# A post-norm decoder layer on one core: who asks for the early loads, whose queue the emptying copies use, and a new order of steps

## The chip, the cores and the metric

One core of a Trainium2 chip. The time is device microseconds from start to end of one launch. Engines: TensorE (PE; PEld is its weight load), VectorE (DVE), ScalarE (ACT), GpSimd (POOL) and SyncE (SP). SP and ACT can both ask the DMA engines for transfers; POOL does so for the indirect ones.

## What is computed

A decoder layer over x of 16 batches x 100 rows x 256 columns: self-attention with rotary turns, cross-attention to the first rows of a context of 16 x 361 x 256, and a mixture of 14 experts with one expert for each row; each part is added to its input and normalised.

```python
x = _layernorm(x + attn(x, qkv_w, qkv_b, out_w, out_b))              # 16 heads of 16, rotary
x = _layernorm(x + xattn(x, ctx, ctx, WQ, bQ, WK, bK, WV, bV, WO, bO, lens))   # 16 heads of 64, causal and padded
x = _layernorm(x + moe(x, router_w, w1, b1, w2, b2))                 # argmax of 14, exact gelu, 256 -> 512 -> 256
```

## The kernel before

The 1,600 rows are cut in two ways: 16 batches b of 100 rows for attention, and 13 tiles t of 125 rows (the last has 100) for loads, projections and norms. Two blocks follow each other. The first does both attentions, the router, and scatters every finished row with its gate and its number to its expert's place in a table in device memory, `expert_rows` (15 x 1,664 rows of 258 words). The second, `experts_block`, loads 128 rows for each expert from that table, runs the two projections and scatters the result to the output.

In the first block the order of all work is a list of 1,715 step names, `STEPS`, written out by hand or by a planner (line 81). Each engine walks the same list (`for step in PLAN: do(step)`), does the steps that are its own and skips the others, so the list fixes the order on each engine; between engines only semaphores wait. Names used below: `xT.t` (PE) turns tile t of x, `xT_hi.t` (ACT) and `xT_lo.t` (DVE) take it as a high and a low part; `w_hi.k` (ACT), `w_lo_v.k` (DVE) or `w_lo_p.k` (POOL) split weight piece k the same way (0, 1: qkv; 2: out; 3, 4: W_K; 5, 6: W_V; 7, 8: W_Q, not split; 9, 10: W_O); `cT.b` turns the context; `v.b`, `qk.t`, `qkT.t`, `K.g.n`, `V.b.c`, `Q.g.n`, `out.t`, `wo.t` are projections and turns on PE; `scores`, `max`, `exp`, `inv`, `norm`, `turn`, `copy_a` or `copy_v` (ACT or DVE), `pv`, `o_hi` (ACT), `o_lo` (DVE) are the steps of attention with side s (self) or x (cross), batch and half; `ln.s.t` ends the self norm of tile t; `x_load.t` and `c_load.b` (SP) load a tile or a batch. The projections on PE share two banks, given out in list order (`banks_in_turn`, line 323).

x lives in a ring of 4 tiles (`XS`), the context in a ring of 2 batches. At the start SP asks for x tile 0, pieces 0 and 1, context 0, pieces 2 to 4, context 1, the biases of K and V, pieces 5 and 6, small tables, pieces 7 to 10 (from line 748). ACT asks beside it for `len_row`, `ident`, the four small inputs `qkv_bias`, `rotary`, `own`, `out_bias` (line 920), which all count to one semaphore `small_in`, and x tiles 1 to 3 (line 922). Later x tiles come by `x_load.t`, which waits for `ln.s.(t-4)`.

The table must hold "no row" where nothing is scattered. Thirteen copies `empty(j)` (line 777) write it from a constant, one slice of 128 rows for each of the 15 parts of the table, 1,935 KB each. SP issues them right behind context loads: j = 0 and 1 behind `c_load.4`, then j = n - 3 behind `c_load.n` (line 789). The scatters wait for them through `emptied`.

Of the kernel before, what the change touches and what calls it, by code (L numbers as in the profile page):

```python
# [86 lines left out]
max.s.0.0.1 qkT_out_a.1 max.s.0.1.0 exp.s.0.0.0 w_lo_p.9 keys_v.1 K.0.2 max.s.0.1.1 qk_out.2 w_hi.10 V.0.0 rot.2
late.0 w_lo_p.10 exp.s.0.0.1 K_out_v.0.2 V_out.0.0 K.0.3 exp.s.0.1.0 mask.0 check.12 inv.s.0.0 mask.1 V.0.1
norm.s.0.0.0 rot_sum.2 exp.s.0.1.1 K_out_v.0.3 norm.s.0.0.1 turn.s.0.0.0 V_out.0.1 check.13 scores.s.1.0
copy_a.s.0.0.0 inv.s.0.1 norm.s.0.1.0 turn.s.0.0.1 max.s.1.0.0 qkT.2 copy_a.s.0.0.1 max.s.1.0.1 norm.s.0.1.1 qk.3  # L90
exp.s.1.0.0 max.s.1.1.0 check.14 qkT_out_v.2 max.s.1.1.1 pv.s.0.0 exp.s.1.0.1 keys_p.2 qk_out.3 turn.s.0.1.0 V.1.0
copy_v.s.0.1.0 check.15 exp.s.1.1.0 inv.s.1.0 rot.3 norm.s.1.0.0 turn.s.0.1.1 o_hi.s.0.0 V.1.1 norm.s.1.0.1
exp.s.1.1.1 o_lo.s.0.0 copy_v.s.0.1.1 V_out.1.0 pv.s.0.1 inv.s.1.1 V_out.1.1 turn.s.1.0.0 norm.s.1.1.0 o_hi.s.0.1
rot_sum.3 v.2 copy_a.s.1.0.0 norm.s.1.1.1 o_lo.s.0.1 turn.s.1.0.1 v_out.2 scores.s.2.0 copy_a.s.1.0.1 pv.s.1.0
max.s.2.0.0 turn.s.1.1.0 o_hi.s.1.0 max.s.2.0.1 exp.s.2.0.0 qkT.3 o_lo.s.1.0 max.s.2.1.0 cT.2 c_load.4
# [1681 lines left out]
```

## Time and profile before

| | us |
|---|---|
| median of 3 runs | 551.65 |
| all runs | 552.34, 548.68, 551.65 |
| the profiled execution, its time | 552.26 |
| its span from first to last instruction | 550.4 |

| engine | busy us | share |
|---|---|---|
| PE | 479.3 | 87% |
| PEld | 405.4 | 74% |
| DVE | 352.6 | 64% |
| ACT | 304.2 | 55% |
| POOL | 216.1 | 39% |

The mean granted TensorE clock is 0.950 of full speed. How to read it: PE is the busiest, but its share is a mean over a start where it has hardly any work, a long middle, and an end with the experts. Rows of the trace are shown in their own section below. SPq and ACTq are DMA requests by SP and ACT; the time beside them is the engine's own time to issue them, not the transfer's.

### The profile page before, as it was taken

How to read it: one execution, taken by the hardware profiler on the slowest of the kernel's cores; microseconds unless marked ns; L12 is line 12 of the kernel's file. 1: busy time of each engine (PE TensorE's matmuls, PEld its weight loads, DVE VectorE, ACT ScalarE, POOL GpSimd, SP SyncE). 2: the span in 40 equal slices, each digit the busy share in tenths (PEclk: the TensorE clock that was granted, in tenths of full speed). 3: DMA queues.
4: the chain of work that ended last, by engine and by line, in shares of the span. 5: the costliest groups of instructions: out<-in, count | busy, mean ns of one | idle time of the engine just before them, and what ended most of it. 6: DMA issues, size and time to landing. Idle time of an engine off the chain costs nothing. (4 is left out here: it accounts for less than half of the span.)

```text
span 550.4 us, 12563 instructions
## 1 busy us (share of the span) xinstructions
PE 479.3 (87%) x4430; PEld 405.4 (74%) x4430; DVE 352.6 (64%) x989; ACT 304.2 (55%) x1417; POOL 216.1 (39%) x296
## 2 busy tenths in 40 slices
PE   0477775989999999999999999999999882899992
PEld 0365564767888878887888888688798771899992
...
GB/s 202 159 175 15 86 323 61 10 11 1 2 153 163 20 108 207 31 11 1 269 46 2 304 21 1 20 298 19 129 27 173 226 8 81 325 371 372 109 24 16
DMA packets 38200, 63.03 MB, mean 115 GB/s; under 512 B 10435, under 2 KB 31412, under 8 KB 37419
## 3 DMA queue, kind: packets, MB, share of 16 engines
...
## 5 line engine op out<-in xcount | busy, mean ns | idle before, releaser
L974 ACT ACTIVATE probs<-bank,neg_max 100x100 f32<-100x100 f32 x512 | 170.2, 377 | 32.1 <-DVE neg_max L1096 24.6
L884 POOL TENSOR_TENSOR probs<-probs,row_inv 100x400 f32<-100x400 f32 x128 | 110.6, 884 | 113.8 <-DVE row_inv L1101 113.5
L974 ACT ACTIVATION_READ_ACCUMULATOR probs<-bank,neg_max 100x1 f32 x512 | 122.3, 240 | 0.0
L1096 DVE TENSOR_REDUCE neg_max<-bank 100x4 f32<-100x400 f32 x128 | 68.0, 565 | 11.8 <-PE bank L1389 5.9
L1400 PE MATMUL bank<-ident,probs 100*100 100x100 f32 x512 | 67.9, 255 | 5.0 <-DVE probsT L1108 2.0
L1400 PEld LDWEIGHTS bank<-ident,probs 100*100 100x100 f32 x512 | 49.8, 130 | 17.7 <-issue 6.2
L983 ACT COPY probsT<-bank 100x400 f32<-100x400 f32 x63 | 31.5, 501 | 40.2 <-PE bank L1400 39.3
L1244 PE MATMUL bank<-cT_h,W_K 128*128 128x200 f32 x256 | 51.5, 288 | 1.6 <-DVE kX L1024 1.5
L1317 PE MATMUL bank<-yT,W_Q 128*128 128x250 f32 (+1 forms) x224 | 50.1, 366 | 1.7 <-DVE yT L1020 1.5
L1108 DVE COPY probsT<-bank 100x400 f32<-100x400 f32 x65 | 37.0, 570 | 17.0 <-PE bank L1400 16.8
L1244 PEld LDWEIGHTS bank<-cT_h,W_K 128*128 128x128 f32 x256 | 42.6, 198 | 3.6 <-DVE kX L1024 1.9
L1244 PE MATMUL bank<-W_O,oX_h 128*125 128x256 f32 (+1 forms) x208 | 42.0, 303 | 2.8 <-DVE oX_l L1117 2.8
L1317 PEld LDWEIGHTS bank<-yT,W_Q 128*128 128x128 f32 x224 | 38.6, 191 | 6.6 <-DVE yT L1020 1.7
L1244 PE MATMUL bank<-W_V,cT_h 128*100 128x512 f32 x128 | 42.0, 409 | 1.5 <-DVE qk L1048 1.5
L1635 ACT ACTIVATE hT<-bank,b1c 128x128 f32<-128x128 f32 x72 | 20.5, 368 | 39.9 <-PE bank L1585 39.9
L1585 PEld LDWEIGHTS bank<-xTs,w 128*128 128x128 f32 x288 | 36.5, 201 | 1.7 <-issue 1.0
L1585 PE MATMUL bank<-xTs,w 128*128 128x128 f32 x288 | 37.0, 285 | 0.4 <-ACT xTs L1625 0.3
L889 POOL TENSOR_TENSOR rstd<-var_eps,half_power 125x1 f32<-125x1 f32 (+1 forms) x26 | 16.1, 618 | 54.2 <-DVE var_eps L1149 54.2
L1244 PEld LDWEIGHTS bank<-W_O,oX_h 128*125 128x125 f32 (+1 forms) x208 | 34.1, 199 | 3.8 <-DVE oX_l L1117 2.3
L1244 PE MATMUL bank<-cT_l,W_K 128*128 128x200 f32 x128 | 35.9, 280 | 0.0
L1244 PE MATMUL bank<-W_self,xT_h 128*100 128x256 f32 (+2 forms) x116 | 32.6, 370 | 3.5 <-DVE W_self L1017 2.2
L1596 PE MATMUL bank<-w,hT 128*128 128x256 f32 x144 | 33.7, 379 | 0.0
...
## 6 DMA issues: line engine op xcount, KB each, us to landing
expert_rows<-c_empty SPq DMA_DIRECT2D x13, 1935.0 KB, 10.0
...
```

The costliest lines, as they stand in the source:

```text
L884: probs_ready.mark(pool.tensor_tensor(v, v, r, ALU.mult), step)
L889: ln_rstd.mark(pool.tensor_tensor(rstd[0:w, s, :], var_eps[0:w, s, :], half_power[0:w, :], ALU.pow), step)
L974: i = act.activation(probs[:, k % SLOTS, w], sc_bank[p % 2 * 2 + u][0:T, w], ACT.Exp, bias=neg_max[:, k % SLOTS, h:h + 1], accum_out=row_s ...
L983: copied[kind].mark(act.copy(probsT[:, k % SLOTS, :], pt_bank[0:T, 0:UW]), step)
L1096: max_ready.mark(dve.tensor_reduce(neg_max[:, k % SLOTS, :], src, AX_X, ALU.max, negate=True), step)
L1108: copied[kind].mark(dve.tensor_copy(probsT[:, k % SLOTS, :], pt_bank[0:T, 0:UW]), step)
L1244: i = pe.matmul(ps, lefts[a][k], rights[b][k], start=(k == 0 and q == 0), stop=(k == n - 1 and q == 2))
L1317: i = pe.matmul(ps[:, h * w:(h + 1) * w], W_Q[:, c, m * P:(m + 1) * P], yT[:, c, 0:w], start=(c == 0), stop=(c == KC - 1))
L1400: i = pe.transpose(pt_bank[0:T, h * T:(h + 1) * T], probs[:, k % SLOTS, h * T:(h + 1) * T], ident[0:T, 0:T])
L1585: i = pe.matmul(h_bank[n % 2][:, f * P:(f + 1) * P], w[:, c, f * P:(f + 1) * P], xTs[:, n % SLOTS_X, c, :], start=(c == 0), stop=(c == KC ...
L1596: i = pe.matmul(y_bank[n % 2][:, 0:D], hT[:, n % SLOTS_X, f, :], w[:, f, :], start=(f == 0), stop=(f == FT - 1))
L1635: i = act.activation(hT[:, n % SLOTS_X, f, :], h_bank[n % 2][:, f * P:(f + 1) * P], ACT.Gelu, bias=bias[f])
```

## The change

Three things. SP asks for x tiles 1, 2 and 3 and the four small inputs, in between its other first loads: x0, pieces 0 and 1, x1, the four small inputs, context 0, x2, pieces 2, 3, 4, context 1, x3, and then as before. ACT no longer asks for them. The copies `empty(j)` are issued by ACT, j = b - 1 directly after `o_hi.s.b.1`, for b = 1 to 13. And `STEPS` is in another order: 522 of 1,715 places differ, most in the first quarter; from `exp.x.11.1.1` on (place 1,406) the two are equal. On PE the first steps become `xT.0 xT.1 cT.0 v.0 v.1 qk.0 xT.2 cT.1 qk.1 qkT.0 K.0.0 xT.3`, where they were `xT.0 xT.1 xT.2 xT.3 v.0 qk.0 v.1 cT.0 cT.1 qk.1 qkT.0 K.0.0`. A few takers change engine (`copy_a` to `copy_v` and the like). No arithmetic is added or removed.

```diff
...
-xT.0 xT_hi.0 bias.s.0 xT_lo.0 xT.1 xT_hi.1 xT_lo.1 xT.2 bias.s.1 xT_hi.2 xT_lo.2 xT.3 w_hi.0 bias.s.2 xT_hi.3
-w_lo_v.0 w_hi.1 check.2 xT_lo.3 bias.s.3 w_lo_v.1 check.3 w_hi.2 v.0 check.4 qk.0 w_lo_v.2 check.5 v_out.0 check.6
...
-turn.s.2.1.1 K.1.0 max.s.3.0.0 x_load.4 copy_a.s.2.1.1 max.s.3.0.1 exp.s.3.0.0 max.s.3.1.0 yT.0 max.s.3.1.1 pv.s.2.1
-bias.x.0 yT_out_a.0 K_out_v.1.0 exp.s.3.0.1 v.4 K.1.1 v_out.4 o_hi.s.2.1 exp.s.3.1.0 inv.s.3.0 o_lo.s.2.1
-norm.s.3.0.0 out.1 K_out_v.1.1 norm.s.3.0.1 exp.s.3.1.1 turn.s.3.0.0 added.s.1 xT.4 copy_v.s.3.0.0 K.1.2 bias.s.4
...
+check.2 check.3 xT.0 check.4 xT_hi.0 bias.s.0 xT_lo.0 check.5 w_hi.0 xT.1 check.6 w_hi.1 w_lo_v.0 bias.s.1 xT_hi.1
+w_lo_v.1 check.7 cT.0 cT_hi.0 c_load.2 xT_lo.1 check.8 cT_lo.0 v.0 check.9 v.1 v_out.0 w_hi.2 check.10 qk.0 v_out.1
...
+norm.s.0.1.1 turn.s.0.0.1 w_hi.9 max.s.1.0.0 qkT.2 max.s.1.0.1 qk.3 copy_a.s.0.0.1 max.s.1.1.0 w_lo_p.9 qkT_out_a.2
...
+norm.s.2.1.0 cT_lo.3 x_load.4 pv.s.2.0 max.s.3.0.0 norm.s.2.1.1 yT.0 o_hi.s.2.0 max.s.3.0.1 exp.s.3.0.0 turn.s.2.1.0
...
+added.s.1 stats.s.1 turn.s.3.0.1 xT.4 copy_a.s.3.0.1 scores.s.4.0 bias.s.4 v_out.4 xT_hi.4 pv.s.3.0 xT_lo.4 rstd.s.1
...
                 load_x(0)
                 for k in range(2):
                     load_piece(k)
+                load_x(1)
+                for dst, src in (
+                    (qkv_bias[:, :], qkv_b.rearrange("(o n) -> o n", o=1).broadcast_to([TT, 3 * D])), (rotary[:, :, :].rearrange("p j w -> p (j w)"), c_rotary),
+                    (own[:, :], c_own), (out_bias[:, :], out_b.rearrange("(o n) -> o n", o=1).broadcast_to([TT, D])),
+                ):
+                    sp.dma_start(dst, src).then_inc(small_in, 16)
                 load_c(0)
+                load_x(2)
                 load_piece(2)
                 for k in (3, 4):
                     load_piece(k)
                 load_c(1)
+                load_x(3)
...
-                def empty(j):
-                    chunk = rows.rearrange("(e j r) w -> e j (r w)", e=NE + 1, r=P)[:, j, :]
-                    sp.dma_start(chunk, c_empty.rearrange("(o r) w -> o (r w)", o=1).broadcast_to([NE + 1, P * ROW])).then_inc(emptied[j // 2], 16)
...
                     elif kind == "c_load":
                         load_c(n)
-                        if n >= 4:
-                            for j in ((0, 1) if n == 4 else (n - 3,)):
-                                empty(j)
...
-                for dst, src in (
-                    (qkv_bias[:, :], qkv_b.rearrange("(o n) -> o n", o=1).broadcast_to([TT, 3 * D])), (rotary[:, :, :].rearrange("p j w -> p (j w)"), c_rotary), (own[:, :], c_own),
-                    (out_bias[:, :], out_b.rearrange("(o n) -> o n", o=1).broadcast_to([TT, D])),
-                ):
-                    act.dma_start(dst, src).then_inc(small_in, 16)
-                for t in range(1, XS):
-                    act.dma_start(xs[:, t, :], x.rearrange("b t d -> (b t) d")[TT * t:TT * (t + 1), :]).then_inc(x_in[t], 16)
+                def empty(j):
+                    chunk = rows.rearrange("(e j r) w -> e j (r w)", e=NE + 1, r=P)[:, j, :]
+                    act.dma_start(chunk, c_empty.rearrange("(o r) w -> o (r w)", o=1).broadcast_to([NE + 1, P * ROW])).then_inc(emptied[j // 2], 16)
...
                         o_high.mark(i, step)
+                        if side == "s" and c == 1 and 1 <= b <= CAP // P:
+                            empty(b - 1)
```

## Rows read from the trace of the kernel before

**Rows 1.** Windows by stage: us, busy by engine (instructions), granted clock, DMA share, GB/s.

```profile
0.00:23.16 23.16, 2.66 (x8) 1.18 (x9) 3.69 (x7) 5.31 (x9) 4.96 (x26) 1.00 0.71 185
23.16:79.80 56.64, 46.78 (x400) 37.24 (x400) 44.94 (x98) 34.16 (x160) 30.13 (x43) 0.94 0.49 137
79.80:88.25 8.45, 0.00 (x0) 0.03 (x1) 1.41 (x7) 0.71 (x5) 0.00 (x0) 0.65 0.59 218
88.25:92.80 4.55, 4.55 (x30) 4.26 (x34) 1.09 (x3) 1.12 (x3) 2.87 (x4) 0.52 0.00 0
92.80:440.00 347.20, 339.85 (x3437) 284.32 (x3430) 250.42 (x693) 231.06 (x1136) 144.09 (x182) 1.00 0.27 90
440.00:469.00 29.00, 14.93 (x97) 12.72 (x95) 10.70 (x50) 5.94 (x16) 5.38 (x8) 0.62 0.16 51
```

**Rows 2.** Waits, 0 to 45 us: engine, line, releaser: us, times, longest.

```profile
PE bank L1277 <- DMA xs<-in_x_dram: 13.0, 3, 10.5
```

**Rows 3.** Timeline of PE, 0 to 45 us: start, us, line, operation, idle before it.

```profile
16.50 0.68 PE L1277 MATMUL bank<-ident,xs 125*128 125x125 f32 x2 [10.51 <-DMA xs<-in_x_dram]
...
20.28 0.65 PE L1277 MATMUL bank<-ident,xs 125*128 125x125 f32 x2 [1.30 <-DMA xs<-in_x_dram]
23.16 0.72 PE L1244 MATMUL bank<-W_self,xT_h 128*100 128x256 f32 x2 [2.23 <-DVE W_self L1017]
...
28.11 0.46 PE L1277 MATMUL bank<-ident,cs 100*128 100x100 f32 x2
...
33.58 0.50 PE L1244 MATMUL bank<-cT_h,W_K 128*128 128x200 f32 x1
...
44.35 0.68 PE L1244 MATMUL bank<-W_V,cT_h 128*100 128x512 f32 x2 [1.54 <-DVE qk L1048]
```

**Rows 4.** Windows of 1 us in the start, columns as in rows 1.

```profile
2.00:3.00 1.00, 0.00 (x0) 0.00 (x0) 0.00 (x0) 0.00 (x0) 0.12 (x2) 1.00 0.64 151
3.00:4.00 1.00, 0.00 (x0) 0.00 (x0) 0.00 (x0) 0.00 (x0) 0.79 (x4) 1.00 0.95 346
...
11.00:12.00 1.00, 0.00 (x0) 0.00 (x0) 0.00 (x0) 0.00 (x0) 0.00 (x0) 1.00 1.21 238
...
17.00:18.00 1.00, 0.17 (x1) 0.00 (x0) 0.39 (x1) 0.37 (x1) 0.72 (x1) 1.00 0.35 108
```

**Rows 5.** Timeline of ACT and its queue, 0 to 58 us.

```profile
3.58 5.14 ACTq L922 DMA_DIRECT2D xs<-in_x_dram  x3
...
39.17 1.05 ACT L929 CAST W_O<-raw_O 128x1024 fp32r<-128x1024 f32 x1 [1.43 <-DMA raw_O<-in_L_xattn_WO_dram]
...
42.84 0.32 ACT L932 ACTIVATE ident_neg<-ident 100x100 bf16<-100x100 f32 x1
...
52.52 0.35 ACT L974 ACTIVATE probs<-bank,neg_max 100x100 f32<-100x100 f32 x1
```

**Rows 6.** Timeline of DVE and of POOL, 0 to 45 us: splitting weights.

```profile
31.14 1.22 DVE L1017 TENSOR_TENSOR W_K<-kX,W_K 128x1024 fp32r<-128x1024 f32 x1
...
31.61 5.49 POOL L858 TENSOR_TENSOR W_V<-qX,W_V 128x1024 fp32r<-128x1024 f32 x2 [3.81 <-ACT W_V L929]
```

**Rows 7.** Waits of 60 to 95 us, columns as in rows 2.

```profile
PE bank L1277 <- DMA xs<-in_x_dram: 8.5, 1, 8.5
```

**Rows 8.** Timeline of SP's queue, 58 to 96 us.

```profile
64.71 1.90 SPq L779 DMA_DIRECT2D expert_rows<-c_empty  x2
67.62 0.35 SPq L746 DMA_DIRECT2D cs<-in_ctx_dram  x1
68.03 0.88 SPq L779 DMA_DIRECT2D expert_rows<-c_empty  x1
73.40 19.92 SPq L735 DMA_DIRECT2D xs<-in_x_dram  x2
```

**Rows 9.** Line 779, all 13 emptying copies: time to issue (ns), time to landing.

```profile
L779 SPq DMA_DIRECT2D expert_rows<-c_empty x13: 859/885/990, 64.7 to 362.1; - x13
...
DMA to landing us min/median/max: 8.4/10.0/19.0
```

**Rows 10.** Waits of PE, 90 to 440 us, the two longest of 11.

```profile
PE bank L1244 <- DVE oX_l L1117: 2.1, 1, 2.1
PE bank L1317 <- DVE yT L1020: 1.5, 1, 1.5
```

More of the change, by code:

```diff
@@ L87 @@
[L87 to L95, printed above, removed]
-copy_v.s.1.1.0 exp.s.2.0.1 qkT_out_v.3 turn.s.1.1.1 max.s.2.1.1 cT.3 keys_p.3 c_load.5 copy_v.s.1.1.1 exp.s.2.1.0
@@ L152 @@
-o_lo.s.8.0 rstd.x.3 cT_lo.7 ln.x.3 turn.s.8.1.1 Q_out_a.2.2 rT.3 copy_v.s.8.1.1 scores.s.9.0 rT_out_a.3 pv.s.8.1
-max.s.9.0.0 logits.3 o_hi.s.8.1 max.s.9.0.1 exp.s.9.0.0 v.10 max.s.9.1.0 o_lo.s.8.1 logits_out.3 v_out.10
-exp.s.9.0.1 out.6 max.s.9.1.1 K.3.0 top.1 added.s.6 exp.s.9.1.0 choose.1 count.1 Q.2.3 K_out_a.3.0 inv.s.9.0
-stats.s.6 norm.s.9.0.0 gate.1 rank.1 norm.s.9.0.1 exp.s.9.1.1 Q_out_v.2.3 turn.s.9.0.0 scores.x.5.0 rstd.s.6 place.1
-copy_a.s.9.0.0 ln.s.6 K.3.1 scatter.2 max.x.5.0.0 x_load.10 inv.s.9.1 max.x.5.0.1 exp.x.5.0.0 scatter.3 turn.s.9.0.1
@@ new lines @@
+inv.s.7.1 choose.0 count.0 norm.s.7.1.0 gate.0 turn.s.7.0.0 qk.7 norm.s.7.1.1 copy_a.s.7.0.0 o_hi.x.3.1 o_lo.x.3.1
+turn.s.7.0.1 qk_out.7 rank.0 copy_a.s.7.0.1 scores.x.4.0 place.0 rot.7 pv.s.7.0 scatter.0 wo.2 o_hi.s.7.0 o_lo.s.7.0
+scatter.1 max.x.4.0.0 max.x.4.0.1 exp.x.4.0.0 rot_sum.7 turn.s.7.1.0 exp.x.4.0.1 added.x.2 qkT.7 copy_v.s.7.1.0 id.2
+V.4.1 qkT_out_v.7 inv.x.4.0 stats.x.2 keys_p.8 turn.s.7.1.1 scores.x.4.1 keys_v.9 copy_a.s.7.1.1 rstd.x.2 V_out.4.1
+norm.x.4.0.0 ln.x.2 pv.s.7.1 max.x.4.1.0 V.5.0 norm.x.4.0.1 o_hi.s.7.1 max.x.4.1.1 exp.x.4.1.0 o_lo.s.7.1 out.5
@@ new lines @@
+choose.1 count.1 Q.2.3 K_out_a.3.0 inv.s.9.0 stats.s.6 norm.s.9.0.0 gate.1 rank.1 norm.s.9.0.1 exp.s.9.1.1
+Q_out_v.2.3 turn.s.9.0.0 scores.x.5.0 rstd.s.6 place.1 copy_a.s.9.0.0 ln.s.6 K.3.1 scatter.2 max.x.5.0.0 x_load.10
+inv.s.9.1 max.x.5.0.1 exp.x.5.0.0 scatter.3 turn.s.9.0.1 K_out_v.3.1 yT.6 scores.x.5.1 copy_v.s.9.0.1 yT_out_a.6
+exp.x.5.0.1 bias.x.6 pv.s.9.0 mask.7 norm.s.9.1.0 K.3.2 max.x.5.1.0 o_hi.s.9.0 o_lo.s.9.0 norm.s.9.1.1 inv.x.5.0
+max.x.5.1.1 norm.x.5.0.0 qk.8 K_out_a.3.2 norm.x.5.0.1 turn.s.9.1.0 qk_out.8 V.6.0 exp.x.5.1.0 copy_v.s.9.1.0 rot.8
@@ new lines @@
+copy_a.s.13.1.1 qk.12 gate.3 inv.s.14.0 Q_out_v.4.3 norm.s.14.0.0 exp.s.14.1.1 norm.s.14.0.1 rank.3 qk_out.12
+pv.s.13.1 place.3 turn.s.14.0.0 o_hi.s.13.1 v.15 copy_a.s.14.0.0 o_lo.s.13.1 scatter.6 inv.s.14.1 rot.12
+turn.s.14.0.1 out.10 copy_a.s.14.0.1 scores.x.10.0 scatter.7 added.s.10 v_out.15 stats.s.10 pv.s.14.0 norm.s.14.1.0
+V.10.1 o_hi.s.14.0 max.x.10.0.0 norm.s.14.1.1 o_lo.s.14.0 exp.x.10.0.0 max.x.10.0.1 rot_sum.12 rstd.s.10
+turn.s.14.1.0 scores.x.10.1 V_out.10.1 copy_a.s.14.1.0 ln.s.10 exp.x.10.0.1 turn.s.14.1.1 max.x.10.1.0 yT.10
@@ new lines @@
+gate.4 choose.4 count.4 pv.x.13.1 K_out_a.7.3 Q.6.1 o_hi.x.13.1 o_lo.x.13.1 rank.4 Q_out_a.6.1 scores.x.14.0 place.4
+wo.10 scatter.8 max.x.14.0.0 max.x.14.0.1 exp.x.14.0.0 scatter.9 exp.x.14.0.1 V.14.1 added.x.10 inv.x.14.0
+stats.x.10 id.10 norm.x.14.0.0 Q.6.2 V_out.14.1 norm.x.14.0.1 turn.x.14.0.0 Q_out_a.6.2 rstd.x.10 scores.x.14.1
+copy_v.x.14.0.0 ln.x.10 turn.x.14.0.1 max.x.14.1.0 rT.10 copy_a.x.14.0.1 max.x.14.1.1 V.15.0 rT_out_a.10
+exp.x.14.1.0 logits.10 V_out.15.0 pv.x.14.0 exp.x.14.1.1 logits_out.10 Q.6.3 o_hi.x.14.0 inv.x.14.1 V.15.1
@@ L240 @@
+norm.x.14.1.0 Q_out_a.6.3 o_lo.x.14.0 norm.x.14.1.1 turn.x.14.1.0 V_out.15.1 scores.x.15.0 copy_a.x.14.1.0
 turn.x.14.1.1 max.x.15.0.0 scores.x.15.1 copy_a.x.14.1.1 max.x.15.0.1 exp.x.15.0.0 pv.x.14.1 max.x.15.1.0
```

270 lines of the change are left out of this document (132 added, 138 removed).

## The prediction

> **What bounds the kernel now.** I read the page first (PE busy 479 of 550.4 us), then windows cut where PE's state changes. They show where PE has no work [rows 1]: in the first 23.16 us it is busy 2.66; from 79.80 to 88.25 it is busy 0.00; from 440 to 469 it is busy 14.93 of 29. From 92.8 to 440 it is busy 339.85 of 347.2, that is 98%, and the longest waits in it are 2.1 and 1.5 us [rows 10]. So PE sets the pace of the long middle, and whatever makes PE arrive earlier at 92.8 moves the end by as much. The tail from 440 on (the last norms, the ranks, the scatters) keeps its steps and its order, and I leave it alone.
>
> The waits name the first gap: 13.0 us of PE for `xs`, the longest 10.5 [rows 2]. The timeline says how: tile 1 is turned at 16.50, tile 3 at 20.28, and because all four turns stand first in PE's order, the first projection starts at 23.16, behind the splitting of weights on DVE [rows 3]. The transfers are the cause: with everything in flight the engines are full (share 0.95 at 346 GB/s; 1.21 at 11 to 12 us), and when mostly x tiles and broadcast biases are left they move 108 GB/s at a share of 0.35, so such loads of 125 rows use a third of the engines [rows 4].
>
> The second gap is one wait: 8.5 us for x tile 4 [rows 7]. SP asked for it at 73.40, behind three emptying copies asked for at 64.71 to 68.9 [rows 8]. One such copy lands 8.4 us after its issue at best and 19.0 at worst [rows 9]. 1,935 KB x 3 from 64.7 to about 88 is 5.9 MB in 23 us, some 255 GB/s, so the tile came out right behind them.
>
> **Early loads.** Removed from ACT: 7 issues, of which the three of x took 5.14 us [rows 5]; ACT idles then anyway, which hides it. Added to SP: the same 7, some 0.3 to 0.6 us each, 3 us in all, beside transfers that are slower than the issues. What counts is the order in one queue. From about 2.2 us on [rows 4], with 108 GB/s for transfers of 125 rows and 336, a little under the 346, for 128 rows: x0, 128,000 bytes, 1.2; pieces 0 and 1, 786 KB, 2.3; x1 1.2; `qkv_bias`, 384,000 bytes, 3.6; `rotary` 0.6; `out_bias` 1.2; context 0, 100 rows, 0.8. Sum 10.9, so context 0 has moved by 13.1 and I add 1 for its completion: 14.1. The other bound is the shared rate of before, where everything to x3 had landed by 20.28 [rows 3]; some two thirds of those bytes stand ahead of context 0, and that gives 13 to 16.
>
> PE's new order is `xT.0 xT.1 cT.0 v.0`. Pieces 0 and 1 are there at 6 to 7 and are split on ACT and DVE while the queue works on the biases, which hides the splitting; then `cT.0` at 14.1 takes 0.5, and `v.0` starts at about 15 in place of 23.16: **8.2 us**. Is it kept? Each later gate, at the old distance from `v.0`:
> - `K.0.0` would be at 33.58 - 8.2 = 25.4 [rows 3]. It needs pieces 3 and 4 and context 1. After 13.1 the queue has x2 1.2, piece 2 0.8, pieces 3 and 4 (1,049 KB at the 238 GB/s of the crowded stretch [rows 4]) 4.4 and context 1 0.8: landed at 20 to 21; then `w_hi.4` 1.05 (the cast of 128x1024 in [rows 5]) and `w_lo_v.4` 1.22 [rows 6]: 23.5. Free by 2 us.
> - `V.0.0` would be at 36.2. Pieces 5 and 6 land by about 29, and POOL's two splits take 5.49 [rows 6]: 35.5. Just free.
> - `late.0` and `w_hi.9` wait for the last inputs, which move no earlier, since the total to transfer is the same. `raw_O` came at 39.17 [rows 5]. Here it matters that `w_hi.9` is moved: it now stands before `exp.s.1.0.0`, which ran at 52.52 [rows 5], so at 44.3. Free. Left in its old place it would have eaten most of the gain.
>
> So 8.2, with bounds 3 (a gate is late) and 10.
>
> **Emptying copies.** Removed from SP: 13 issues of 0.885 us, hidden before. The 8.45 us stall goes: on ACT's queue `empty(0)` follows `o_hi.s.1.1`, `x_load.4` comes some 5 us later, and in the new order 12 PE steps stand between `ln.s.0` and `xT.4` (8 before, `K.1.2` and a turn among the new ones), about 10 us of work. A copy that lands in 8.4 to 10 us leaves 5 at most after `x_load.4` is issued. **8.45 us**, bounds 4 and 8.45. With the gap goes what followed it: from 88.25 to 92.80 PE was busy all 4.55 us at a granted clock of 0.52, close to its 1.2 GHz level, having idled 8.45 before [rows 1]. At full clock the same takes 4.55 x 0.52 = 2.4: **2.2 us**. What is late next is DVE, 80% busy in the stretch ahead of the gap (44.94 of 56.64); it needed only 1.41 more in the gap to catch up, so at most that is given back.
>
> The Trainium skill, "DMA: Bandwidth & Descriptors", section "Issuing engines are not separate DMA queues", says that DMAs of the scalar, sync and gpsimd engines run on the same 16 DMA engines and interleave, whoever started them. By it a change of queue alone frees no bandwidth, and tile 4 would come when the copy in flight does; by the rows that is the 5 us above, still hidden, so the sum stays and the rule feeds a rival below.
>
> Added to ACT: 13 issues, 13 x 0.885 = 11.5 us [rows 9], each directly after an `o_hi`, with the next `exp`, copy or cast of ACT queued behind it, and for those DVE's `inv`, POOL's `norm` and PE's `turn` wait. Bounds: 0, if ACT's idle third hides it (busy 231 of 347 [rows 1]), and 11.5. PE hardly waits in the middle [rows 10], so there is slack; the first four copies (b = 1 to 4) fall where PE idles 10 of 57 us for its neighbours. I take half of those, 1.8, and a tenth of the other nine, 0.8: **minus 2.6**.
>
> **Other moves.** Same instructions, other places; takers swapped between ACT and DVE cost the same on either (0.5 us or so). They fill up to 10 us of small PE idles before 79.8, or open new ones: 0, bounds -2 and +3.
>
> **Sum.** 8.2 + 8.45 + 2.2 - 2.6 = 16.3. The profiled execution: 550.4 - 16.3 = 534.1 of span, 536.0 with the 1.9 around it; its 552.26 stands 0.6 above the median of 551.65. From the median: 535.4.
>
> **Rivals.**
> - *The single queue gives back the start.* Everything early now passes one queue; the context stands behind 576 KB that use a third of the engines, and if `cT.0` comes at 16 and the W_V splits end at 39, only 2 to 3 us of 8.2 remain. For: 108 GB/s [rows 4], and V's gate has 0.7 us of room. Against: x1 to x3 used the same engines before. Time 551.65 - 16.3 + 5.5 = 541. Chance 0.14.
> - *Tile 4 is still late.* By the rows, two copies in flight land up to 19.0 us after issue [rows 9]; if `empty(1)` overlaps the tile's transfer on the same engines, tile 4 is 3 to 8 us late: 539 to 545. The skill's rule on shared DMA engines is this case. Against: the copies are now one for each batch. Chance 0.07.
> - *ACT's issues are exposed in full*: 11.5 for 2.6, time 544. Chance 0.08.
> - *Slower: ACT is held while it issues.* When the queues were full, three issues on ACT took 5.14 us, 1.7 each [rows 5]. If each empty held ACT by that much more than 0.885 and all of it reached PE, 13 x 1.7 = 22 against 18.9 gained: 555. It decides from 1.45 us a copy, fully exposed. Against: the 13 issues on SP took 0.990 at most, also with two in flight [rows 9]. Chance 0.04.
> - *The forecast*, 529 to 539: chance 0.67.
>
> **How the numbers follow.** About 1%, or 5.5 us, is what a measurement of this kernel can tell from no change, so faster means below 546.1. Forecast 0.67, the first rival 0.14, nearly all of the second and most of the third are faster: 0.88. Same: 0.08, from the ends of the second and third and the near side of the fourth. Slower: 0.04. The range goes from 529 (10 from the start, nothing exposed on ACT, some small idles filled: 551.65 - 10 - 8.45 - 2.2 - 2) to 543 (the first rival and part of the second or third); outside it is about 2 in 10.
>
> **What would show it.** Right: the first W_self matmul at 14 to 16 us; `K.0.0` near 25; no wait of PE for `xs` above 1 us between 50 and 100; PE's 0.52 stretch gone; 13 ACTq issues of about 0.9 us; PE busy total hardly changed but 2 us. Wrong: a wait of PE for `cs` beyond 16 us or of the first projections on W_K or W_V splits; `xs` again in PE's waits; PE waits on ACT's probabilities after each `o_hi.s`; ACTq issues of 2 us and more. The largest single risk is the FIFO estimate of 14.1 us.

## The result, and the profile after

| | before | after |
|---|---|---|
| median, runs of one comparison | 552.0 (4 runs) | 532.95 (4 runs, 530.44 to 537.1) |
| ratio, 95% interval | | 0.966 [0.957, 0.975] |
| the same kernels in a later comparison | 553.52 | 532.33, ratio 0.963 [0.957, 0.970] |
| span of the profiled execution | 550.4 | 530.4 |
| first mask matmul (L1384 before, L1383 after) starts | 108.1 | 91.8 |
| last mask matmul starts | 432.3 | 416.0 |
| last router matmul (`Wr`) starts | 459.1 | 439.6 |

Some runs fall into a slower state of the chip, whatever the kernel; the ratios and medians from here on leave them out.

The change makes the kernel 19 us faster; 535.4 (529 to 543) was forecast. The four milestones say where: 16.3 us are won by the first mask matmul, nothing between the first and the last (324.2 us before and after), 3.2 between there and the last router matmul, 0.5 behind it.

The page's busy line of the kernel after, PE first: PE is busy 4.6 us less than before, in a span shorter by 20.

```profile
PE 474.7 (90%) x4430; PEld 401.6 (76%) x4430; DVE 352.8 (67%) x989; ACT 305.0 (58%) x1417; POOL 215.5 (41%) x296
```

The timeline of PE, 0 to 80 us (start, us, line, operation, idle before it and what ended it), answers to [rows 3]:

```profile
14.18 0.58 PE L1276 MATMUL bank<-ident,cs 100*128 100x100 f32 x2 [5.82 <-DMA cs<-in_ctx_dram]
14.46 0.73 PE L1243 MATMUL bank<-W_self,xT_h 128*100 128x256 f32 x2
...
27.02 0.51 PE L1243 MATMUL bank<-cT_h,W_K 128*128 128x200 f32 x1
...
36.30 0.67 PE L1243 MATMUL bank<-W_V,cT_h 128*100 128x512 f32 x2 [0.29 <-DVE qk L1047]
...
76.89 0.38 PE L1276 MATMUL bank<-ident,xs 125*128 125x125 f32 x2
```

PE now turns x tiles 0 and 1, waits 5.8 us for context 0, and begins the projections at 14.46 where it was 23.16. The last line is tile 4, turned without a wait, where [rows 7] had one of 8.5 us. The waits of PE, 0 to 100 us (engine, line, releaser: us, times, longest), say the same; they answer to [rows 2, 7]:

```profile
PE bank L1276 <- DMA cs<-in_ctx_dram: 7.6, 2, 5.8
...
PE bank L1243 <- DVE xT_l L1033: 2.4, 1, 2.4
...
PE bank L1276 <- DMA xs<-in_x_dram: 1.5, 1, 1.5
```

The windows of the kernel after, columns as in [rows 1] (us, then busy us of PE, PEld, DVE, ACT, POOL, granted clock, DMA share, GB/s): the start, then a stretch behind the small waits of 58 to 63 us, the middle, and from the last mask matmul to the last router matmul:

```profile
0.00:14.46 14.46, 1.64 (x6) 0.89 (x7) 2.57 (x4) 3.48 (x5) 2.66 (x21) 1.00 0.58 174
...
68.00:70.00 2.00, 2.00 (x11) 2.00 (x11) 1.25 (x3) 2.00 (x14) 0.00 (x0) 0.50 0.04 8
...
91.80:416.00 324.20, 320.65 (x3250) 268.12 (x3249) 236.81 (x658) 216.84 (x1062) 137.42 (x172) 1.00 0.26 87
416.00:439.60 23.60, 15.39 (x143) 13.29 (x142) 9.56 (x37) 9.97 (x45) 7.19 (x10) 0.88 0.47 166
```

A stretch at clock 0.50 is still there, from 62 to 72 us, behind PE's idles of 58 to 63.

The emptying copies on ACT's queue, all 13 (issue time in ns, min, median and max; start of the first and the last; landing in us), answer to [rows 9]:

```profile
L919 ACTq DMA_DIRECT2D expert_rows<-c_empty x13: 852/861/966, 58.0 to 325.8; - x13
...
DMA to landing us min/median/max: 8.2/9.0/10.9
```

An issue takes as long as on SP (0.86 for 0.885 us). The landing that took up to 19.0 us takes 10.9 at most. ACT's timeline around the first of them shows what an issue costs the engine itself:

```profile
58.01 0.97 ACTq L919 DMA_DIRECT2D expert_rows<-c_empty  x1
...
58.52 0.27 ACT L989 CAST oS_h<-bank 128x100 fp32r<-128x100 f32 x1
59.03 0.34 ACT L971 ACTIVATE probs<-bank,neg_max 100x100 f32<-100x100 f32 x1 [0.24 <-issue]
```

Here the queue is ahead of the engine: while it issues from 58.01 to 58.98, ACT works off what was queued before, until 58.79, the cast `o_hi` that stands ahead of the issue in the program among it. Of 0.97 us ACT stands still 0.24. But this is the best case. Where ACT has waited for PE just before the cast, nothing is queued, and the issue starts with the cast. The last of the 13, on ACT and then on PE, is of this kind:

```profile
325.80 0.24 ACT L989 CAST oS_h<-bank 128x100 fp32r<-128x100 f32 x1 [0.21 <-PE bank L1417]
325.81 0.86 ACTq L919 DMA_DIRECT2D expert_rows<-c_empty  x1
326.71 0.49 ACT L980 COPY probsT<-bank 100x400 f32<-100x400 f32 x1 [0.67 <-PE bank L1399]
```

```profile
327.34 0.52 PE L1399 MATMUL bank<-ident,probs 100*100 100x100 f32 x4 [0.41 <-ACT probsT L980]
```

The issue ends at 326.67 and the copy starts at 326.71. The profile puts the 0.67 us of idle down to PE, whose turn came in while ACT stood; the kernel with the copies on SP behind x tiles (below) has the same two instructions 0.45 us apart and not 0.91, and there PE does not wait for the copy:

```profile
323.13 0.24 ACT L991 CAST oS_h<-bank 128x100 fp32r<-128x100 f32 x1 [0.21 <-PE bank L1417]
323.58 0.49 ACT L982 COPY probsT<-bank 100x400 f32<-100x400 f32 x1 [0.21 <-PE bank L1399]
```

At nine of the 13 issues ACT's next instruction starts 0.04 to 0.11 us after the issue has ended, with 0.24 to 0.72 us of idle before it: 5.4 us in all, where the same instructions idle 1.3 us with the copies on SP.

### The profile page after: what moved, and what is told of

Same layout as the page of the kernel before. It is cut to its first block and busy times, and to the rows that moved or that the text cites. A ratio compares the mean times of both kernels' runs of the same rounds, so it can differ in the third digit from the quotient of the medians.

```text
span 530.4 us, 12558 instructions
## 1 busy us (share of the span) xinstructions
PE 474.7 (90%) x4430; PEld 401.6 (76%) x4430; DVE 352.8 (67%) x989; ACT 305.0 (58%) x1417; POOL 215.5 (41%) x296
## 5 line engine op out<-in xcount | busy, mean ns | idle before, releaser
L980 ACT COPY probsT<-bank 100x400 f32<-100x400 f32 x65 | 32.6, 502 | 40.1 <-PE bank L1399 39.2
L1107 DVE COPY probsT<-bank 100x400 f32<-100x400 f32 x63 | 35.9, 570 | 15.2 <-PE bank L1399 14.9
L1243 PE MATMUL bank<-W_O,oX_h 128*125 128x256 f32 (+1 forms) x208 | 40.1, 293 | 2.4 <-DVE oX_l L1116 2.4
L1584 PEld LDWEIGHTS bank<-xTs,w 128*128 128x128 f32 x288 | 36.2, 199 | 1.7 <-issue 1.0
L1243 PEld LDWEIGHTS bank<-W_O,oX_h 128*125 128x125 f32 (+1 forms) x208 | 32.6, 191 | 3.9 <-DVE oX_l L1116 2.3
```

Of the source, the lines that this page charges most:

```text
L980: copied[kind].mark(act.copy(probsT[:, k % SLOTS, :], pt_bank[0:T, 0:UW]), step)
L1107: copied[kind].mark(dve.tensor_copy(probsT[:, k % SLOTS, :], pt_bank[0:T, 0:UW]), step)
L1243: i = pe.matmul(ps, lefts[a][k], rights[b][k], start=(k == 0 and q == 0), stop=(k == n - 1 and q == 2))
L1584: i = pe.matmul(h_bank[n % 2][:, f * P:(f + 1) * P], w[:, c, f * P:(f + 1) * P], xTs[:, n % SLOTS_X, c, :], start=(c == 0), stop=(c == KC ...
```

## The experiments

Three edits make the change, and the forecast gave each its own term. The first four kernels take them apart; the rest measure the costs in dispute. Each kernel was timed beside the kernel before.

| kernel | median | ratio [95%] | span | first W_self | tile 4's wait | first to last mask matmul |
|---|---|---|---|---|---|---|
| before | 552 to 554 | 1 | 550.4 | 23.16 | 8.45 | 108.1 to 432.3: 324.2 |
| loads only | 554.29 | 1.002 [0.997, 1.008] | 554.7 | 25.59 | 8.92 | 114.0 to 438.2: 324.2 |
| copies on ACT only | 546.01 | 0.988 [0.982, 0.994] | 544.0 | 23.02 | none | 100.4 to 425.8: 325.4 |
| order only | 539.46 | 0.975 [0.969, 0.981] | 538.9 | 19.60 | 3.25 | 100.2 to 422.3: 322.1 |
| order and loads | 532.05 | 0.962 [0.955, 0.970] | 530.2 | 14.20 | 2.84 | 94.1 to 416.2: 322.1 |
| after | 532.95 | 0.966 [0.957, 0.975] | 530.4 | 14.46 | none | 91.8 to 416.0: 324.2 |

**The loads alone.** The kernel before, with SP's first loads as in the change and nothing else.

```diff
                     load_piece(k)
+                load_x(1)
+                for dst, src in (
...
+                ):
+                    sp.dma_start(dst, src).then_inc(small_in, 16)
                 load_c(0)
+                load_x(2)
...
                 load_c(1)
+                load_x(3)
```

> The kernel before, with the early loads asked for by SP in the new order, and nothing else changed. My theory, that the start gains only where PE's order also lets the first projection go before x tiles 2 and 3: PE still turns all four tiles first, tile 3 is now the last of the early loads and lands at 20 to 22 us, so the first projection starts at 23 to 25 us (23.16 before), the wait for tile 4 near 80 us stays, and the ratio to the kernel before is 1.00 (0.995 to 1.005). Rival, that the order in the queue is worth its 8 us by itself: first projection near 15 us and a ratio of 0.985.

Measured 554.29, ratio 1.002 [0.997, 1.008]. The timeline of PE, 13 to 95 us, shows why nothing is won: the old order has all four turns ahead of the first projection, and in one queue x tile 3 comes last of the four.

```profile
14.85 0.65 PE L1277 MATMUL bank<-ident,xs 125*128 125x125 f32 x2 [6.40 <-DMA xs<-in_x_dram]
22.71 0.65 PE L1277 MATMUL bank<-ident,xs 125*128 125x125 f32 x2 [7.21 <-DMA xs<-in_x_dram]
25.59 0.72 PE L1244 MATMUL bank<-W_self,xT_h 128*100 128x256 f32 x2 [2.23 <-DVE W_self L1017]
...
92.89 0.65 PE L1277 MATMUL bank<-ident,xs 125*128 125x125 f32 x2 [8.92 <-DMA xs<-in_x_dram]
```

Loads in the order of use help only an order that uses them so. Tile 4's wait does not go with them.

**The copies alone.** The kernel before, with `empty(b - 1)` issued by ACT behind `o_hi.s.b.1`.

```diff
-                        if n >= 4:
-                            for j in ((0, 1) if n == 4 else (n - 3,)):
-                                empty(j)
...
                         o_high.mark(i, step)
+                        if side == "s" and c == 1 and 1 <= b <= CAP // P:
+                            empty(b - 1)
```

> The kernel before, with the emptying copies issued by ACT behind o_hi.s.b.1, old order of steps, old early loads. My theory: the 8.5 us wait of PE for x tile 4 goes, with the slow-clock stretch behind it, and ACT's 13 issues give back 0 to 3: 8 to 10.6 us less, ratio 0.981 to 0.986. Rival 1, that a copy in flight on the other queue holds the tile on the same DMA engines: here only 8 PE steps (about 7 us) stand between the load and its use, so a wait of 1 to 4 us for tile 4 stays, ratio 0.985 to 0.99. Rival 2, that ACT's issues are exposed in full: 11.5 us back, ratio 1.00.

Measured 546.01, ratio 0.988 [0.982, 0.994]; the span is 6.4 shorter. PE's turn of tile 4 comes at 82.37 with no wait, where [rows 7] had 8.5:

```profile
82.37 0.38 PE L1276 MATMUL bank<-ident,xs 125*128 125x125 f32 x2
```

The middle takes 1.2 us more than before. In the old order, then, moving the copies takes away the stall, as the forecast had it. The gain is 7.7 us at the first mask matmul and not the 8.45 and more that was expected: PE reaches tile 4 only at 82.37, where it was ready at 79.80, and the stretch of slow clock ahead of it lasts from 69 to 76 us and not from 69 to 72.

**The order alone.** The kernel before with the new list of steps; loads and copies as before.

```diff
-xT.0 xT_hi.0 bias.s.0 xT_lo.0 xT.1 xT_hi.1 xT_lo.1 xT.2 bias.s.1 xT_hi.2 xT_lo.2 xT.3 w_hi.0 bias.s.2 xT_hi.3
...
+check.2 check.3 xT.0 check.4 xT_hi.0 bias.s.0 xT_lo.0 check.5 w_hi.0 xT.1 check.6 w_hi.1 w_lo_v.0 bias.s.1 xT_hi.1
...
```

> The kernel before, with the new list of steps alone; early loads and emptying copies asked for as before. My theory: the first projection no longer waits for x tiles 2 and 3 but still for tile 1 (turned at 16.5 us), so it starts at 17 to 18 us, 5 us earlier; tile 4 still comes out behind three copies, but 10 us of work in place of 7 stand between its load and its use, so 4 to 5 us of the 8.5 stay: some 9 us less, ratio 0.98 to 0.987. Rival, that the better packing of the steps is the gain and the transfers matter little: ratio 0.97 or lower.

Measured 539.46, ratio 0.975 [0.969, 0.981]: some 13 us, the largest share of the change. The timeline of PE has two of its reasons:

```profile
17.93 0.68 PE L1277 MATMUL bank<-ident,xs 125*128 125x125 f32 x2 [11.37 <-DMA xs<-in_x_dram]
19.60 0.72 PE L1244 MATMUL bank<-W_self,xT_h 128*100 128x256 f32 x2 [0.67 <-DVE xT_l L1034]
...
83.64 0.40 PE L1277 MATMUL bank<-ident,xs 125*128 125x125 f32 x2 [3.25 <-DMA xs<-in_x_dram]
```

The first projection starts 3.6 us earlier, with ACT still asking for x1 in the crowd. And tile 4 is waited for 3.25 us, not 8.45, although the copies stand on SP as before: the order puts more of PE's work ahead of that turn. The tile itself is as late as ever: from SP's request to PE's turn it takes 15.2 us (68.43 to 83.64), where it took 14.9 (73.40 [rows 8] to 88.25). The third is the middle, 322.1 for 324.2. The expectation missed on both sides: the first projection came later than its 17 to 18 us, the wait was shorter than its 4 to 5, and the ratio lies between its 0.98 and the rival's 0.97.

**Order and loads, the copies left on SP.** The changed kernel with the copies behind the context loads on SP.

```diff
                     elif kind == "c_load":
                         load_c(n)
+                        if n >= 4:
+                            for j in ((0, 1) if n == 4 else (n - 3,)):
+                                empty(j)
```

> The changed kernel with its emptying copies put back on SP's queue behind the context loads. My theory: the start stays as in the changed kernel (first projection at 14.5 us), and the wait for tile 4 comes back, shorter than the 8.5 us of before since more work stands ahead of its use: 4 to 6 us, with some slow clock behind it, so 5 to 7 us slower than the changed kernel, ratio to before 0.975 to 0.982. Rival, that moving the copies was worth nothing: ratio 0.966 as the changed kernel's.

Measured 532.05, ratio 0.962 [0.955, 0.970], against 0.966 and 0.963 for the changed kernel: moving the copies brings nothing that can be measured once the order is new. That was the rival; the theory wanted a wait of 4 to 6 us and 5 to 7 us of time. SP's queue (the last copy ahead of the tile, and the tile) and PE's turn show the stall that is left, and the two kinds of price are in the windows of the middle and at the tile:

```profile
57.85 0.86 SPq L787 DMA_DIRECT2D expert_rows<-c_empty  x1
62.91 0.30 SPq L735 DMA_DIRECT2D xs<-in_x_dram  x1
```

```profile
77.65 0.41 PE L1277 MATMUL bank<-ident,xs 125*128 125x125 f32 x2 [2.84 <-DMA xs<-in_x_dram]
```

```profile
94.10:416.20 322.10, 320.07 (x3250) 268.05 (x3248) 235.42 (x658) 216.76 (x1062) 137.36 (x172) 1.00 0.26 87
```

With the copies on ACT the first mask matmul is 2.3 us earlier (91.8 for 94.1) and the middle 2.1 longer (324.2 for 322.1): 0.2 is left at the last mask matmul.

**The changed kernel again**, unaltered, beside the next kernels.

> The changed kernel itself, unchanged, on the chip of the next three, so that they can be set against it: ratio to the kernel before 0.966, and 324 us between the first and the last mask matmul of PE (line 1383).

Measured 532.33, ratio 0.963 [0.957, 0.970], span 531.5; first to last mask matmul 91.6 to 414.9, 323.3 us. So the middle of the same kernel varies by 0.9. All kernels with the new order and copies of one kind agree on ACT's price there: with the copies on ACT the middle takes 323.3, 323.4 and 323.3 us in three (this one and two below) and 324.2 in the first profile, with the copies on SP 322.0 to 322.1 in four. PE's waits for ACT in the middle are 1.4 us in each of the first four and 0.3 in each of the last; the first profile has two more waits of PE, of 0.4 and 0.3 us, that the profile lays to no other engine. The price is 1.2 to 1.4 us, and 2.1 in that one profile.

**The copies on SP, each behind an x tile.** Neither ACT nor a tile should pay.

```diff
                         load_x(n)
+                        for j in {4: (0,), 5: (1,), 6: (2, 3), 7: (4,), 8: (5,), 9: (6, 7), 10: (8, 9), 11: (10, 11), 12: (12,)}[n]:
+                            empty(j)
```

> The changed kernel with its 13 emptying copies issued by SP, each behind an x load (so never ahead of the one that is needed next) and none by ACT. Theory A, formed after the first four runs: moving the copies to ACT saves a wait of 2.8 us for tile 4 and costs some 2.1 us later, because ACT issues them; here both are gone. No wait for tile 4, first to last mask matmul 322 us (not 324), 2 us less than the changed kernel, ratio to before 0.960 to 0.963. Rival B, that the 2.1 us come from the transfers themselves beside the work or from chance: still 324 us there, ratio as the changed kernel's.

Measured 533.32, ratio 0.963 [0.955, 0.971], span 532.2. There is no tile wait and the middle takes 322.0 (91.3 to 413.3), both as wanted, and yet the end is no earlier. The stretch from the last mask matmul to the last router matmul, the same 142 to 145 matmuls in each kernel, has the reason; the kernel before, this one, order with loads, and 112 and 13 rows (below):

```profile
432.30:459.10 26.80, 19.27 (x143) 16.91 (x142) 9.64 (x37) 10.09 (x45) 7.23 (x10) 0.72 0.41 148
```

```profile
413.30:440.10 26.80, 19.27 (x143) 16.92 (x142) 9.65 (x37) 10.09 (x45) 7.23 (x10) 0.72 0.42 150
```

```profile
416.20:439.20 23.00, 14.80 (x145) 12.79 (x142) 9.57 (x37) 9.97 (x45) 7.19 (x10) 0.93 0.48 169
```

```profile
410.90:433.00 22.10, 13.90 (x144) 11.82 (x142) 9.53 (x37) 9.99 (x45) 7.20 (x10) 0.96 0.52 178
```

The work is the same and the waits are alike; PE's busy time goes from 13.90 us at a granted clock of 0.96 to 19.27 at 0.72. Here PE idles in small pieces, and how much of the stretch is run at the lower of its two levels differs from kernel to kernel (and in the changed kernel from 0.88 to 0.77 between its two profiles). That is 4.7 us between the extremes, more than the 1.2 to 2.1 in dispute. Why a kernel gets the one or the other was not found.

**The copies doubled.** Each copy is made twice, the second into a spare table; nothing else differs from the changed kernel.

```diff
                             empty(b - 1)
+                            chunk = spare_rows.rearrange("(e j r) w -> e j (r w)", e=NE + 1, r=P)[:, b - 1, :]
+                            act.dma_start(chunk, c_empty.rearrange("(o r) w -> o (r w)", o=1).broadcast_to([NE + 1, P * ROW])).then_inc(spared, 16)
```

> The changed kernel with each of ACT's 13 emptying copies followed by a second one into a spare table that nobody reads (work added: 13 issues and 25 MB). Theory A: each issue on ACT exposes about 0.16 us, since ACT's queue runs ahead of its engine; with 1.7 us for two in a row in place of 0.86 more is exposed, 2 to 6 us more in all, ratio to before 0.970 to 0.978. My recorded price (a fifth or so of 0.885 exposed) gives 2.6 more. Rival, full exposure: 11.5 us more, ratio 0.987. If the transfers matter and not the issues, x tile waits show up in PE's waits.

Measured 558.99, ratio 1.011 [1.003, 1.019], 27 us more than the changed kernel beside it (532.33) and far from every forecast. One tile carries most of it. SP asks for tile 5 at 80.63, behind four copies; PE turns it at 117.01, after a wait of 18.85:

```profile
117.01 0.65 PE L1281 MATMUL bank<-ident,xs 125*128 125x125 f32 x2 [18.85 <-DMA xs<-in_x_dram]
```

```profile
100.00:112.00 12.00, 0.00 (x0) 0.00 (x0) 0.00 (x0) 0.00 (x0) 0.00 (x0) 0.59 0.90 319
112.00:116.00 4.00, 0.00 (x0) 0.00 (x0) 0.00 (x0) 0.00 (x0) 0.00 (x0) 0.50 0.36 157
```

The windows show the engines full until 112 and the traffic thin from there: the tile came out only when the copies asked for behind it, at 85.33 to 98.38, had gone through as well. So the rival "tile 4 is still late" of the prediction is a real mechanism; it came with 3.9 MB a batch in place of 1.9, and nothing between was tried.

**Doubled copies, x tiles in 112 and 13 rows.** Is it the backlog, or the shape of the tile's transfer?

```diff
+def halves_of(n):
+    return (0, n // 16 * 16), (n // 16 * 16, n)
...
-                    sp.dma_start(xs[0:size(t), t % XS, :], x.rearrange("b t d -> (b t) d")[TT * t:TT * t + size(t), :]).then_inc(x_in[t % XS], 16)
+                    for a, b in halves_of(size(t)):
+                        sp.dma_start(xs[a:b, t % XS, :], x.rearrange("b t d -> (b t) d")[TT * t + a:TT * t + b, :]).then_inc(x_in[t % XS], 16)
```

> The kernel with doubled copies (13 more of 1,935 KB into a spare table, on ACT's queue), and the x tiles alone asked for in two parts of 112 and 13 rows. Theory A (shared by packets): the copies move in packets of 30 KB, a tile of 125 rows in packets of 1 KB on about a third of the engines, so a tile waits behind one large packet for each of its rows on an engine; over all engines it has a third of the rows on each. Tile 6, which took 26 us from its request to PE's turn, then lands within about 10 us, the wait of 18.9 us falls to 3 at most, and the time comes to 534 to 542 us. Theory B (backlog): the tile comes when the copies asked for ahead of it and beside it have gone through, whatever its shape; the wait stays within 3 us of 18.9, and the time is 555 to 559.

Measured 552.96, ratio 0.997 [0.991, 1.002]. What the expectation calls tile 6, with 26 us, is tile 5 by the count of the turns, and took 36.4 from request to turn (80.63 to 117.01). Here it is asked for at 78.38 and turned at 101.28, 22.9 us later, in the middle of traffic that goes on beyond 112:

```profile
101.28 0.65 PE L1286 MATMUL bank<-ident,xs 125*128 125x125 f32 x2 [5.39 <-DMA xs<-in_x_dram]
```

```profile
100.00:112.00 12.00, 7.67 (x46) 6.39 (x46) 6.11 (x17) 3.59 (x18) 2.89 (x4) 0.73 0.87 293
```

A backlog that passes any tile by alike (theory B) is out: the same copies stood ahead and beside, and the tile got through 13.5 us sooner, ahead of the last of them. But theory A is no more than half right: a third of the rows on an engine should have given a third of the time and 534 to 542, and gave two thirds of it. The middle takes 345.8 us, 22.5 more than the 323.3 of the changed kernel's second profile: 10.7 are three waits for tiles, the longest 5.4; 6.8 are PE's busy time (327.8 for 321.05 us), run at a lower clock behind the waits; and 5 are left, which the next kernel explains. How the tile's packets and the copies' share an engine was not settled.

The Trainium skill, "DMA: Bandwidth & Descriptors", section "Why a DMA increments its semaphore by 16 and not by 1", says that a DMA runs on the largest number of engines up to 16 that divides its slowest dimension. By it 125 rows run on 5 engines and 112 on 16. This case's rows agree: a share of 0.35 while loads of 125 rows were left [rows 4], and the shorter time here.

**A second issue without the bytes.** Behind each copy ACT asks for one of 1 KB for each part of the spare table.

```diff
                             empty(b - 1)
+                            chunk = spare_rows.rearrange("(e j r) w -> e j (r w)", e=NE + 1, r=P)[:, b - 1, 0:ROW]
+                            act.dma_start(chunk, c_empty.rearrange("(o r) w -> o (r w)", o=1)[:, 0:ROW].broadcast_to([NE + 1, ROW])).then_inc(spared, 16)
```

> The changed kernel with one more DMA behind each of the 13 emptying copies on ACT's queue, of 1 KB to each expert's part of a spare table: the issue without the bytes. Theory A (what ACT pays is the issue): 13 issues more cost the middle, from the first mask matmul to the last, as much again as the first 13 did, if each takes as long: 323.3 to 324.2 becomes 325 to 326, the time 533 to 536 us. Theory B (ACT's queue runs ahead of its engine, and what the middle pays is the large transfers or nothing): 323 to 324.2 and 531 to 533.5. An issue much shorter than the 0.86 us of a copy leaves A no more than its share of 2.

Measured 538.54, ratio 0.974 [0.969, 0.980], 5 to 6 us more than the changed kernel; first to last mask matmul 93.3 to 422.2, 328.9 us, for 323.3 to 324.2. It is the issue that costs (theory A), and it costs more than A said. The small copies' issues, then the same copy on ACT and the same turn on PE as shown above for one issue and for none:

```profile
L998 ACTq DMA_DIRECT2D spare_rows<-c_empty x13: 805/806/897, 61.1 to 332.2; - x13
```

```profile
333.07 0.49 ACT L982 COPY probsT<-bank 100x400 f32<-100x400 f32 x1 [1.53 <-issue]
```

```profile
333.71 0.52 PE L1404 MATMUL bank<-ident,probs 100*100 100x100 f32 x4 [1.28 <-ACT probsT L982]
```

With no issue ACT idles 0.21 us here, with one 0.67, with two 1.53; PE waits 0, 0.41 and 1.28. The issue of 15 KB in all takes 0.81 us where that of 1,935 KB takes 0.86, so the bytes hardly matter. At the nine places where one issue held ACT, the idle grows from 5.4 to 13.3 us, 0.88 for each issue added; the profile itself names the issue as the cause at seven places only, 10.3 us, and lays the other two to DVE. To ACT the second issue costs what the first does. To PE it costs more: 4.7 to 5.6 us in the middle for the second 13, 1.2 to 2.1 for the first, as if the first had used up most of the slack.

**The early loads in 112 and 13 rows.** The changed kernel with x tiles, `qkv_bias`, `rotary` and `out_bias` cut in this way.

> The changed kernel with every x load, qkv_bias, rotary and out_bias cut in two: 112 rows and 13 rows, in place of 125. Theory: loads of 125 rows move at 108 GB/s on a third of the DMA engines and those of 112 rows on all; the 7.8 us that they take ahead of context 0 shrink to about 2.6, so cT.0 is at 9 to 10 us in place of 14.2 and the whole kernel is 3 to 5 us faster than the changed one if the W_K and W_V splits follow: ratio to before 0.957 to 0.961. Rival: the next gate (issue of more transfers by SP, W_K on the same engines, DVE's rotary work) takes it back: cT.0 earlier, but K.0.0 still at 27 us and the ratio as before.

Measured 527.04, ratio 0.957 [0.949, 0.966], span 523.9. PE's timeline:

```profile
7.63 0.68 PE L1283 MATMUL bank<-ident,xs 125*128 125x125 f32 x2 [3.36 <-DMA xs<-in_x_dram]
10.81 0.58 PE L1283 MATMUL bank<-ident,cs 100*128 100x100 f32 x2 [2.50 <-DMA cs<-in_ctx_dram]
11.09 0.73 PE L1250 MATMUL bank<-W_self,xT_h 128*100 128x256 f32 x2
...
33.56 0.68 PE L1250 MATMUL bank<-W_V,cT_h 128*100 128x512 f32 x2 [0.29 <-DVE qk L1054]
```

Context 0 is turned 3.4 us earlier, `V.0.0` runs 2.7 earlier and the first mask matmul 4.3 (87.5 for 91.8). The changed kernel, in the same comparison, had 532.33 (its four runs 531.03 to 533.32, these 525.41 to 531.53): 5 us less, though the two intervals of the ratio still overlap, [0.949, 0.966] and [0.957, 0.970].

**Both: 112 and 13 rows, the copies on SP behind x tiles.**

> The kernel with loads in 112 and 13 rows, its 13 emptying copies back on SP, each asked for behind an x tile in place of ahead of one. Theory A (ACT's 13 issues cost 1 to 2 us of the middle and the end takes them over): 525 to 526, against 527.0. Theory B (as in the run with the copies behind the tiles and whole loads: the 2 us of the middle are given back in the tail after the last mask matmul): 526.5 to 528, with the last mask matmul near 409 and the last router matmul where it was.

Measured 528.93, ratio 0.955 [0.948, 0.961], span 527.0. The ratio and the medians do not tell it from the last. The last mask matmul starts at 409.0, the last router matmul at 435.9, and the 26.9 us between them were run at a clock of 0.72: theory B, that the tail gives back the 2 us, but through its clock.

**112 and 13 rows, context 0 ahead of the biases.**

```diff
                 load_x(1)
+                load_c(0)
                 for dst, src in (
                     (qkv_bias, ...), (rotary, ...), (out_bias, ...)
...
-                load_c(0)
                 load_x(2)
```

> The kernel with the early loads in 112 and 13 rows, and context 0 asked for directly behind x tile 1, ahead of the broadcast biases. Theory A (each early gate is where its transfer stands in the one queue, and the first projection's gain reaches the end): the turn of context 0 moves from 10.81 to 8 to 9, the first W_self matmul from 11.09 to 9 to 10, and the time falls by 1 to 2, to 525 to 526. Theory B (the gates behind it, the splitting of W_K and W_V, stay where they are): the first W_self matmul moves as well, but V.0.0 stays near 33.6 and the time near 527. In either case the ratio to the kernel before stays below that of the changed kernel, 0.965.

Measured 526.08 (524.64 to 530.87), ratio 0.959 [0.950, 0.967], span 524.2. It ran on another chip than the others, so only the ratio can be set beside theirs.

```profile
7.64 0.58 PE L1283 MATMUL bank<-ident,cs 100*128 100x100 f32 x2
8.79 0.72 PE L1250 MATMUL bank<-W_self,xT_h 128*100 128x256 f32 x2 [0.57 <-DVE xT_l L1040]
...
17.86 0.54 PE L1283 MATMUL bank<-ident,cs 100*128 100x100 f32 x2 [3.23 <-DMA cs<-in_ctx_dram]
...
21.87 0.33 PE L1250 MATMUL bank<-cT_h,W_K 128*128 128x200 f32 x1
...
32.82 0.63 PE L1250 MATMUL bank<-W_V,cT_h 128*100 128x512 f32 x2
```

The first projection is 2.3 us earlier, and PE then waits 3.2 for context 1, which has not moved; `K.0.0` is 2.5 earlier all the same (21.87 for 24.39; why, is said under "Start" below), and 0.7 is left at `V.0.0`, at the first mask matmul (86.8 for 87.5) and at the last (410.1 for 410.9), and none in the ratio (0.959 for 0.957). Behind the first gate the next one stands, so theory B holds for `V.0.0` and the time. This kernel and the two before it were compared once each; all three intervals lie below 0.967.

## Why the prediction was right, and where it was not

The total was right. Of the signs that the text named, the first projection (14.46 for 14 to 16), the missing wait for tile 4 and the 13 issues of 0.86 us are there; `K.0.0` is 1.6 us late, PE's busy time fell by 4.6 and not by 2, and a stretch of slow clock is left. Its terms, against the profiles:

| term | forecast | measured |
|---|---|---|
| start | 8.2 | 8.7 at the first projection, 6.6 at `K.0.0`, 8.05 at `V.0.0` |
| tile 4's stall | 8.45 | 8.45 gone: 5.2 to 5.6 by the order, 2.8 to 3.3 by the copies |
| the slow clock | 2.2 | about -1.0, in the second profile +0.6 |
| ACT's 13 issues | -2.6 | -1.2 to -1.4 in the middle, -2.1 in the first profile |
| order of steps otherwise | 0 | 2.1 in the middle |
| the tail | 0 | 3.2, in the second profile 1.4 |

They add up to 18.7 with the -2.1 and the 3.2 (8.05 + 8.45 - 1.0 - 2.1 + 2.1 + 3.2), against 20.0 between the spans. Of the other 1.3, 0.5 stand behind the last router matmul; 0.8 ahead of the first mask matmul were not traced. That the total came so close is in part luck: the clock fell 3.2 short of its term, and 2.1 in the middle and 1.4 to 3.2 in the tail, both put at 0, made up for it.

**Start.** Context 0 was to be there at 14.1 and was turned at 14.18; the sum over one queue, transfer by transfer with 108 and 336 GB/s, held to 0.1 us, with the 1 us for completion that the text had chosen and not read. `K.0.0` came at 27.02 and not at 25.4: not for its pieces, which had "free by 2 us", but for DVE, where rotary products and the low part of tile 2 stood ahead and PE waited 2.4 us for `xT_l`. One of the two rotary products took 2.57 us where others take 0.42, beside a split of W_K on POOL; the timelines of DVE (both products in one line) and of POOL:

```profile
19.66 3.04 DVE L1063 TENSOR_TENSOR rot<-qk,rotary 125x256 f32<-125x256 f32 x2
```

```profile
19.87 2.53 POOL L859 TENSOR_TENSOR W_K<-kX,W_K 128x1024 fp32r<-128x1024 f32 x1
```

The long one starts at 20.1 and ends 0.3 us after POOL's split. It is long in the same way in the kernel before (2.60 us from 34.8 on, beside the splits of W_V [rows 6]) and in four more kernels with the new order; with context 0 ahead of the biases the product does not meet a split, takes 0.75 us at most, and `K.0.0` comes 2.5 us earlier (the products start 1.5 us earlier there, too). That DVE waits for POOL here is read from these coincidences; no edit tested it. `V.0.0` at 36.30 met the 36.2. The text looked for the late gate among the transfers and the splits of weights; it was DVE's queue, and two thirds of the loss were caught up by `V.0.0`. The three kernels with parts of the change show what the text only implied: the loads without the order bring nothing (ratio 1.002), the order without the loads 3.6 of the 8.7.

**Tile 4.** The size was right and the cause half wrong. The text put all 8.45 us to the copies' leaving SP, and counted the steps now standing ahead of `xT.4` ("12 PE steps, 8 before") only as the cover for one copy. Those steps alone take off 5.2 (order only, 3.25 left) to 5.6 us (order and loads, 2.84 left), while the tile is no earlier. A stall that two edits each could end was credited to one. Had the forecast asked, as it should, what each edit does with the other in place, it would have given the move of the copies 2.8 gained less what ACT pays: 1 to 2 us, too little to be seen, which is what the ratios 0.962 and 0.966 say.

**The clock.** The step "with the gap goes what followed it" failed. The stretch behind tile 4's gap is gone, but the one behind the small idles at 58 to 63 us is longer: 62 to 72 us at 0.50, where before it was about 69 to 72. In the kernel after some 9.4 us of PE's busy time were run there at half speed, 4.7 of them lost (in its second profile 6.2 and 3.1); before, about 1.5 near 70 and 2.2 behind the gap [rows 1]. So the clock takes 1.0 more in this stretch than before, or 0.6 less by the second profile, in no case 2.2 less, and gives 1.4 to 3.2 in the tail, which the text had left alone.

**ACT's issues.** Taking half the price for four copies and a tenth for nine gave 2.6; the middle showed 1.2 to 1.4, once 2.1. So the term was of the right kind and about twice too large. The reasoning, that ACT's idle third hides the issues, holds only in part: at nine of 13 places ACT is held until its issue is done, 5.4 us of idle where there were 1.3, and PE's waits for ACT in the middle rise from 0.3 to 1.4 us. Most of it is absorbed between ACT and PE. With two issues in a row PE pays 4.7 to 5.6 us more for 10.5 us of issuing; the sum's bound of 11.5 is for a kernel without slack.

**Order otherwise.** It was put at 0 with -2 to +3; 2.1 in the middle lies in it, as fewer and shorter idles of PE (322.1 us from mask to mask, 320.07 of them busy, against 319.70 busy of 324.2).

**The rivals.** *The single queue gives back the start* did not come: it needed context 0 at 16. *Tile 4 still late* did not, but doubled copies bring it on (18.85 us). *ACT held while it issues*, by 1.7 us a copy, did not: ACT is held, but the longest of the 13 issues took 0.966 us. *Exposed in full* did not either: of 11.2 us of issuing 1.2 to 2.1 reached PE.
